# Routing the mixture's rows by a table of tokens, with gathers from GpSimd

## The reference

```python
rn = (xf - mu) * rsqrt(var + EPS) * ln_gamma + ln_beta
probs = softmax(rn @ gate_w.T)
rw, sel = top_k(probs, 2)
comb = sum(one_hot(sel, 8) * rw[..., None], axis=1)
h = gelu(einsum('nc,efc->enf', xf, w1))       # w1: 8 x 1024 x 512
y = einsum('enf,ecf->enc', h, w2)             # w2: 8 x 512 x 1024
x = x + einsum('enc,ne->nc', y, comb)
```

## Time and profile before

| | us |
|---|---|
| median of 3 runs (1031.40 to 1032.46) | 1031.93 |
| profiled execution, device time | 1033.27 |
| its span in the profile | 1031.5 |
| PE busy | 913.2 (89%) |
| DVE busy | 686.1 (67%) |
| ACT busy | 527.9 (51%) |
| POOL busy | 407.2 (39%) |

### The profile page before, as it was taken

The page is one execution under the profiler, slowest core; times in us unless marked ns, Lnnn a source line. Parts: engine busy times, 40 slices in busy tenths (PEclk is TensorE's granted clock), DMA queues, the critical chain, the costliest instruction groups (busy, mean ns, idle before and its releaser), DMA issues. The chain is left out here.

```text
span 1031.5 us, 24517 instructions
## 1 busy us (share of the span) xinstructions
PE 913.2 (89%) x10397; PEld 611.0 (59%) x10397; DVE 686.1 (67%) x1010; ACT 527.9 (51%) x801; POOL 407.2 (39%) x293
## 2 busy tenths in 40 slices
PE   5988999999999999999999999767775495899996
PEld 3464676676676676676676676433443383676663
DVE  7854777646777645777644455775667495799983
ACT  3543445555345545345544345531554562899893
POOL 2020665355665355665345545422230074111112
PEclk9998999999999999999999999669997597999999
DMA  9361122443022332022332022007600355999993
GB/s 340 103 180 42 33 61 60 126 105 89 22 59 63 124 105 54 20 56 63 124 106 53 22 54 62 2 1 263 270 2 1 129 212 171 414 400 398 400 391 45
DMA packets 48455, 134.63 MB, mean 131 GB/s; under 512 B 9870, under 2 KB 11790, under 8 KB 44506
## 3 DMA queue, kind: packets, MB, share of 16 engines
q1 hardware_dynamic: 45356, 126.78, 36.1%
q0 software_dynamic: 2800, 6.04, 2.9%
q10 hardware_dynamic: 192, 0.26, 0.1%
HBM read 94.99 MB, written 11.33 MB: 103 GB/s over the span
## 5 line engine op out<-in xcount | busy, mean ns | idle before, releaser
L419 POOL TENSOR_TENSOR acc_pool<-acc_pool,pT 128x1024 f32<-128x1024 f32 x92 | 216.7, 2355 | 170.2 <-ACT pT L688 168.5
L688 ACT ACTIVATE pT<-ps_s 128x1024 f32<-128x1024 f32 x128 | 130.7, 1021 | 216.7 <-PE ps_s L857 216.4
L526 DVE TENSOR_REDUCE mpart<-ps_b 128x1 f32<-128x512 f32 x256 | 174.4, 686 | 94.7 <-PE ps_b L835 93.6
L819 PE MATMUL ps_a<-wv_hi,cT_hi 128*128 128x128 f16 x1024 | 184.4, 220 | 0.4 <-ACT kbias L608 0.4
L821 PE MATMUL ps_a<-wv_hi,cT_lo 128*128 128x128 f16 x1024 | 183.3, 219 | 0.0
L820 PE MATMUL ps_a<-wv_lo,cT_hi 128*128 128x128 f16 x1024 | 183.2, 219 | 0.0
L521 DVE TENSOR_TENSOR k_lo<-k_f,k_hi 128x512 f16<-128x512 f32 x64 | 72.3, 1129 | 70.2 <-ACT k_hi L664 69.9
L835 PE MATMUL ps_b<-k_stack,q_stack 98*128 98x512 f16 x256 | 98.6, 388 | 11.9 <-DVE mpart L526 7.7
L819 PEld LDWEIGHTS ps_a<-wv_hi,cT_hi 128*128 128x128 f16 x1024 | 99.7, 97 | 12.4 <-issue 11.9
L857 PE MATMUL ps_s<-q_stack,k_stack 98*128 98x128 f16 x1024 | 100.2, 227 | 7.3 <-ACT pT L688 6.2
L820 PEld LDWEIGHTS ps_a<-wv_lo,cT_hi 128*128 128x128 f16 x1024 | 100.2, 98 | 5.0
(11 more groups left out here) (248 smaller groups left out, 1873.9 us busy)
## 6 DMA issues: line engine op xcount, KB each, us to landing
w_raw<-in_w SPq DMA_DIRECT2D x30, 2048.0 KB, 16.8
raw<-in_context SPq DMA_DIRECT2D x16, 1024.0 KB, 5.8
k_stack<-k_hi SPq DMA_DIRECT2D x252, 64.0 KB, 2.0
k_stack<-k_lo SPq DMA_DIRECT2D x128, 64.0 KB, 2.0
slots_in<-a_zeros SPq DMA_DIRECT2D x1, 3855.0 KB, 13.6
rows_in<-slots_in SPq DMA_DIRECT2D x15, 257.0 KB, 16.3
q_stack<-k_stack SPq DMA_DIRECT2D x12, 128.0 KB, 2.4
x_sb<-in_x SPq DMA_DIRECT2D x2, 512.0 KB, 4.1
```

The lines of the kernel that those rows point to most:

```text
L419: nc.gpsimd.tensor_tensor(acc_pool[:, :], pT[:, 0, :] if p == 1 else acc_pool[:, :], pT[:, p % PT, :], ALU.add).then_inc(pool_add, 1)
L526: nc.vector.tensor_reduce(mpart[:, j, kb:kb + 1], bank_b(step)[:, :], AX.X, ALU.max).then_inc(p1_max, 1)
L688: nc.scalar.activation(pT[:, p % PT, :], ps_s[:, :], ACT.Exp, scale=SM_SCALE).then_inc(exp_done, 1)
L819: nc.tensor.matmul(to, cT_hi[:, c, keys], t.wv_hi[:, c, col], start=(c == 0), stop=False)
```

## The change

The features no longer travel with the record. What changes:

- `normed` rows are stored to a new table `rows` in memory, in token order: three blocks during self-attention, the fourth at the start of the mixture, and one block of zeros for the spare token (5 stores of 256 KB).
- The record of a slot is 2 floats, weight and token. The same eight scatters write them into `slots` (1920 x 2 floats), which was filled beforehand from an 8-byte constant per partition.
- POOL waits for the eight, reads `slots` back into one SBUF tile `table` with a plain DMA of its own (128 partitions x 15 tiles x 2 floats), and then gathers each tile's 128 rows out of `rows` by the token column, four tiles ahead.
- SP no longer waits for `sent` and no longer loads rows.
- `y_evict(k - 2)` stands behind `w2_high(k)` in ACT's loop, waits for `table` once, and has three buffers `y`.
- The copy `second` is gone, and so is the load of the spare token's number into the zeros: `misc_in` counts to 5.

```diff
-ROWS_RING = 8
-RECORD = D + 2
+ROWS_RING = 6
+Y_RING = 3
...
# self-attention, SP
-            sp.dma_start(t.normed[:, :, D + 1], io.tokens[:, 0:NB], allow_slow_non_contiguous=True).then_inc(s.tokens_in, 16)
             sp.wait_ge(zeroed, 1)
-            sp.dma_start(io.out[NB * P:NB * P + P, :], zeros[:, 0:D]).then_inc(s.out_sem, 16)
-            sp.dma_start(zeros[:, D + 1:D + 2], io.tokens[:, NB:NB + 1], allow_slow_non_contiguous=True).then_inc(misc_in, 16)
-            sp.wait_ge(misc_in, 16 * 6)
-            sp.dma_start(io.slots_in.rearrange("(n p) d -> p n d", p=P),
-                         zeros[:, :].unsqueeze(1).broadcast_to([P, TILES, RECORD])).then_inc(s.slots_zeroed, 16)
+            sp.dma_start(io.out[NB * P:NB * P + P, :], zeros[:, :]).then_inc(s.out_sem, 16)
+            sp.dma_start(io.rows[NB * P:NB * P + P, :], zeros[:, :]).then_inc(s.rows_stored, 16)
+            sp.dma_start(io.slots.rearrange("(n p) r -> p n r", p=P), io.empty.unsqueeze(1).broadcast_to([P, TILES, 2])
+                         ).then_inc(s.slots_empty, 16)
...
+            for d in range(NB - 1):
+                sp.wait_ge(m_normed, 2 * d + 1)
+                sp.dma_start(io.rows[P * d:P * (d + 1), :], t.normed[:, d, :]).then_inc(s.rows_stored, 16)
...
# self-attention, POOL and DVE
-            v.wait_ge(misc_in, 16 * 6)
+            v.wait_ge(misc_in, 16 * 5)
...
# mixture, SP
+            sp.wait_ge(normed, 2 * NB)
+            sp.dma_start(io.rows[P * EARLIER:P * NB, :], t.normed[:, EARLIER, :]).then_inc(s.rows_stored, 16)
...
             w2_load(2)
-            sp.wait_ge(sent, 16 * 2 * NB)
-            for k in (*range(EARLY, ROWS_AHEAD), *range(EARLY)):
-                rows_load(k)
             experts_of_further_tiles()
-            for k in range(TILES):
-                if k + ROWS_AHEAD < TILES:
-                    rows_load(k + ROWS_AHEAD)
-                if 4 <= k + 3 < TILES:
+            for k in range(1, TILES):
+                if k + 3 < TILES:
                     w1_load(k + 3)
-                if 3 <= k + 2 < TILES:
+                if k + 2 < TILES:
                     w2_load(k + 2)
...
# mixture, POOL
+            def gather(k):
+                if k >= EARLY + ROWS_RING:
+                    pool.wait_ge(x_tr, k - ROWS_RING + 1)
+                nc.gpsimd.indirect_dma_start(
+                    out=rows_in[k % ROWS_RING][:, :], out_offset=None, in_=io.rows, in_offset=token(k),
+                    bounds_check=NB * P + P - 1).then_inc(rows_got[k % ROWS_RING], 16)
...
+            pool.wait_ge(sent, 16 * 2 * NB)
+            pool.dma_start(table[:, :, :], io.slots.rearrange("(n p) r -> p n r", p=P)).then_inc(table_in, 16)
+            pool.wait_ge(s.rows_stored, 16 * (NB + 1))
+            pool.wait_ge(table_in, 16)
+            for k in range(EARLY, ROWS_AHEAD):
+                gather(k)
             pool.wait_ge(s.out_sem, 16 * (NB + 1))
             for k in range(TILES):
+                if k + ROWS_AHEAD < TILES:
+                    gather(k + ROWS_AHEAD)
                 pool.wait_ge(y_out, k + 1)
                 if k:
                     pool.wait_ge(y_added, 16 * k)
...
# mixture, ACT
             def y_evict(k):
                 act.wait_ge(down, k + 1)
-                if k < EARLY:
-                    act.wait_ge(rows_got[k], 16)
-                if k >= 2:
-                    act.wait_ge(y_added, 16 * (k - 1))
+                if k == 0:
+                    act.wait_ge(table_in, 16)
+                if k >= Y_RING:
+                    act.wait_ge(y_added, 16 * (k - Y_RING + 1))
...
             for k in range(TILES):
-                if k >= 2:
-                    y_evict(k - 2)
...
                 if k:
                     w2_high(k)
+                if k >= 2:
+                    y_evict(k - 2)
                 if k + 2 < TILES:
                     w1_high(k + 2)
```

More of the change, by code:

```diff
@@ L946, in self_attention @@
         m_hat, gT = sb("am_hat", [P, D]), sb("am_gT", [P, NC, P])
-        zeros = sb("a_zeros", [P, RECORD])
+        zeros = sb("a_zeros", [P, D])
         ps_p = ctx.enter_context(nc.psum_tensor("a_psp", [P, HEADS, P], F32))
@@ L1367, in mixture @@
                         for half in (t.cT_hi, t.cT_lo)]
-        rows_in = [sb(f"rows_in{u}", [P, RECORD]) for u in range(ROWS_RING)]
+        rows_in = [sb(f"rows_in{u}", [P, D]) for u in range(ROWS_RING)]
         xT_hi, xT_lo = [[sb(f"m_xT_{half}{u}", [P, NC, P], F16) for u in range(2)] for half in ("hi", "lo")]
@@ L1371, in mixture @@
         h_hi, h_lo = [[sb(f"h_{half}{u}", [P, NF, P], F16) for u in range(2)] for half in ("hi", "lo")]
-        y = [sb(f"m_y{u}", [P, D]) for u in range(2)]
-        second = sb("m_second", [P, NB, RECORD])
+        y = [sb(f"m_y{u}", [P, D]) for u in range(Y_RING)]
+        records, table = sb("m_records", [P, 2, NB, 2]), sb("m_table", [P, TILES, 2])
         stats, mv, rstd = sb("m_stats", [P, 6]), sb("m_mv", [P, 2]), sb("m_rstd", [P, 2])
@@ L1485, in _, with token @@
             nc.gpsimd.memset(ones[:, :], 1.0).then_inc(const_in, 1)
-            pool.wait_ge(s.slots_zeroed, 16)
-            pool.wait_ge(rowed, 1)
-            pool.wait_ge(s.tokens_in, 16 * 2)
-            for k, records in enumerate((t.normed, second)):
-                for b in range(NB):
-                    if k:
-                        pool.wait_ge(copied, NB + b + 1)
-                    nc.gpsimd.indirect_dma_start(
-                        out=io.slots_in, out_offset=bass.IndirectOffsetOnAxis(ap=rows[:, k, b:b + 1], axis=0),
-                        in_=records[:, b, :], in_offset=None, bounds_check=TILES * P - 1).then_inc(sent, 16)
+            def token(k):
+                return bass.IndirectOffsetOnAxis(ap=table[:, k, 1:2].bitcast(mybir.dt.uint32), axis=0)
+            def gather(k):
[4 more added lines that the diff above has]
+                    bounds_check=NB * P + P - 1).then_inc(rows_got[k % ROWS_RING], 16)
+            pool.wait_ge(s.slots_empty, 16)
+            pool.wait_ge(rowed, 1)
+            for b in range(NB):
+                for k in range(2):
+                    nc.gpsimd.indirect_dma_start(
+                        out=io.slots, out_offset=bass.IndirectOffsetOnAxis(ap=rows[:, k, b:b + 1], axis=0),
+                        in_=records[:, k, b, :], in_offset=None, bounds_check=TILES * P - 1).then_inc(sent, 16)
+            pool.wait_ge(sent, 16 * 2 * NB)
[4 more added lines that the diff above has]
+                gather(k)
             pool.wait_ge(s.out_sem, 16 * (NB + 1))
             for k in range(TILES):
+                if k + ROWS_AHEAD < TILES:
+                    gather(k + ROWS_AHEAD)
                 pool.wait_ge(y_out, k + 1)
@@ L1502, in _ @@
                     pool.wait_ge(y_added, 16 * k)
-                token = rows_in[k % ROWS_RING][:, D + 1:D + 2].bitcast(mybir.dt.uint32)
                 nc.gpsimd.indirect_dma_start(
-                    out=io.out, out_offset=bass.IndirectOffsetOnAxis(ap=token, axis=0), in_=y[k % 2][:, :],
+                    out=io.out, out_offset=token(k), in_=y[k % Y_RING][:, :],
                     in_offset=None, bounds_check=NB * P + P - 1, compute_op=ALU.add).then_inc(y_added, 16)
@@ L1529, in _ @@
             v.wait_ge(powed, 3 * NB)
-            for k, dst in ((1, hat[:, :]), (0, t.normed[:, last_b, 0:D])):
+            for k, dst in ((1, hat[:, :]), (0, t.normed[:, last_b, :])):
                 nc.vector.tensor_scalar(dst, t.x[:, last_b, :], mv[:, 0:1], rstd[:, k:k + 1],
@@ L1608, in _ @@
             then_wait(nc.vector.tensor_reduce(rows_f[:, :, :], placed[:, :, :, :], AX.X, ALU.add))
-            for k, records in enumerate((t.normed, second)):
-                nc.vector.tensor_scalar(records[:, :, D], weight[:, k, :], UNSCALE, None, ALU.mult)
+            nc.vector.tensor_scalar(records[:, :, :, 0], weight[:, :, :], UNSCALE, None, ALU.mult)
             nc.vector.tensor_copy(rows[:, :, :], rows_f[:, :, :]).then_inc(rowed, 1)
@@ L1702, in _ @@
             w1_high(1)
-            for b in range(1, NB):
-                second_copy(b)
             x_high(0)
             for k in range(TILES):
-                if k >= 2:
-                    y_evict(k - 2)
                 for i in range(2):
@@ L1884 @@
     tiles = np.asarray(inputs["ctx_1024"]).reshape(NB * NKT, P, D)
+    tokens = np.zeros((P, NB + 1, 2), np.uint32)
+    tokens[:, :, 1] = np.arange((NB + 1) * P).reshape(NB + 1, P).T
     arrays = {
@@ L1904 @@
         "before": np.ascontiguousarray(np.stack([np.triu(np.ones((P, P)), 1), np.ones((P, P))], axis=1).astype(np.float16)),
-        "tokens": np.ascontiguousarray(np.arange((NB + 1) * P, dtype=np.uint32).reshape(NB + 1, P).T).view(np.float32),
+        "records": np.ascontiguousarray(np.tile(tokens[:, None, 0:NB, :], (1, 2, 1, 1))).view(np.float32),
+        "empty": np.ascontiguousarray(tokens[:, NB, :]).view(np.float32),
         "counting": np.tile(np.concatenate([np.arange(MORE), P * np.arange(EXPERTS),
```

37 lines of the change are left out of this document (15 added, 22 removed).

## The result

| | before | after |
|---|---|---|
| median of 4 runs, us | 1032.20 (1031.40 to 1033.62) | 1055.55 (1051.17 to 1059.03) |
| profiled execution, us | 1033.27 | 1051.17 |
| its span, us | 1031.5 | 1049.4 |

After takes 1.0223 times as long, 95% interval 1.0181 to 1.0264. Slower was forecast, but by 3 us and within 1047; it is 23 us in the medians and 17.9 us between the two profiled spans. Those 17.9 us can be divided into four stretches of PE's stream. The profiled execution is the fastest of after's four, and that of before lies 1.1 us above its median, so the medians lie further apart than the spans; where the other executions of after lose their 3 to 8 us no trace shows.

What follows compares the result with a forecast made beforehand. The prediction took the DMA engines to bound the middle, PE only 0.4 us a tile behind. Terms -2.4 + 2 + 6.1 - 6.6 + 4.1 = +3.2 us gave a median of about 1035 us; 8 in 10: 1024 to 1047.

Steps and rivals of the forecast that it cites:

- Self-attention, minus 2.4: Self-attention: DVE's first bias addition no longer waits for the spare token's number; the stage moves 2.4 us earlier, bounds 0 and 4.
- The scatters, plus 2: Routing scatters: still eight with POOL's times as before, but the last three land beside weights; 2 us more, bounds 0 and 4.
- Table and gather, plus 6.1: Start of tile 3: two dependent transfers, table load then gather, take 9.1 us against 3.0 for the row load before.
- The table's pieces: Rival, slower: POOL builds the table load's 1920 pieces at scatter pace, 13.5 us more, median about 1049; chance 0.15.
- The stream after it, minus 6.6: Tile 3's transposes to last up product: with a lead in weights PE is the bound, 133.1 us instead of 139.75.
- the third rival: Slower: gathers and results on POOL wait for pauses in DVE's splits, results remain for the end; about 1042, chance 0.12.
- POOL falls behind in the stream: Rival, slower: gathers and results wait for pauses in DVE's splits; end 11 us late instead of 4, about 1042; chance 0.12.
- The results, plus 4.1: End of the kernel: result 12 leaves later behind ACT's last weight split, the last results follow serially in 6.15 us steps.
- The scatters are not held: Rival, faster: fifth and sixth scatters wait for at most one 2.3 us DVE instruction; median about 1023; chance 0.17.

Runs made afterwards that it cites:

- the spare token's experiment: Kernel before, with the load of the spare token's number counted on another semaphore, so VectorE's first bias addition does not wait for it: 0.9986.
- results unchained: Changed kernel, each tile's result written plainly to its own table, without adding or waiting for the landing of the one before: 1.0006, 1031.0 us.
- weights first: Kernel before, with SP issuing w1 of tile 4, w2 of tile 3 and w1 of tile 5 ahead of its wait for the scatters: 1.0036, 1035.46 us.
- pauses: Kernel before, with a one-column VectorE memset behind each weight split of the first tiles: 0.9981, 1027.58 us.
- all three repairs: Changed kernel, gathers seven tiles ahead, `y_evict` ahead of the gelu, VectorE waiting before w2_low(0) until the eight scatters are issued: 0.9972, 1030.73 us.

## Why the prediction was wrong, point by point

*Self-attention, minus 2.4.* The term looks right in the table and was not. The wait went as said, but by the spare token's experiment the gain is given back within self-attention. After's own trace shows the same. DVE starts its first normalisation there at 693.72 instead of 695.92, so 2.2 us early, in code that was not touched. It is 4.4 us early at the first bias addition (701.81), 3.4 at the next (713.87), 3.1 at 729.72, and 2.2 again at 764.39 and at the start of the mixture. So after's 2.2 us stem from before self-attention, and that they nearly equal the forecast is luck; what gave them no run shows. The prediction moved the stage whole ("the stage moves with it"), having read one wait and not the next ones. Its lower bound, 0, is what happened.

*The scatters, plus 2.* Same two holds, of 9.89 and 10.91 us. The 1.2 us more of the sixth and a landing of 6.19 instead of 2.77 us beside the weights make 4.6, over the stated bound of 4. The size was short, the mechanism right (making VectorE wait removes the holds).

*Table and gather, plus 6.1* (its heading says 6.2). From the last landing (865.03) to PE's start it took 8.83 us, 3.0 before: plus 5.8. The table's pieces are no cost: 1.28 us. By the Trainium skill's rule that descriptors are cheap to build ("DMA: Bandwidth & Descriptors", section "Anatomy of one DMA — SWDGE (gpsimd) path"), the sum stayed as it was; the trace agrees for this load.

*The stream after it, minus 6.6.* This is the step that failed, by 11.4 of the 14.7 us between the forecast and the spans. "PE is then the bound" looked only at weights, PE and DVE. It forecast 133.1 us and after took 144.5. Two things were wrong in it, in opposite directions. PE's own step is 10.98 us and not 11.35: seven of after's eleven steps are 10.98 to 11.04, and all eleven with gathers seven ahead. The prediction took 11.35 from PE's busy time and from one step of before, and neither was PE's need. That alone would have made the stream 8.3 + 11 x 10.98 = 129.1 us, and with gathers seven ahead it is 128.6, so the part about the weights' lead held. The other four steps of after hold its four later waits for rows, 11.5 us, and about 4 us more. Of these 3.6 lie behind the two longest waits (steps of 15.68 and 19.18 us around waits of 2.80 and 6.47), where the clock was near half. That 144.5 less 11.5 is again 133.0 is chance: the slow clock and the step that was taken too long happen to be of one size. What was missed is that rows, until then loaded by SP ahead of the weights of the tile before, now sat in POOL's stream behind a wait for a landing. A gather for tile k + 5 is issued when result k has been sent. Result 7 leaves at 975.40, so the gather of tile 12 goes at 977.29, and PE is then at tile 11 (978.24). Results take 11.4 to 14.6 us a step while weights move, and a gather another 9 to 14. Every number for that was in the rows: results landing in 10.9 us, plus 0.8 of POOL, against PE's 11.35. The prediction used them for the third rival and there asked only what stays over for the end. *POOL falls behind in the stream* named the right cause ("a step of results is ... already more than PE's 11.35") and put the price in the wrong place: in the tail, which came out at 4.8 us instead of 11, and not in the rows, and it had 0.12. Where PE no longer waits for rows, with gathers seven ahead, the tail is 10.8 us longer than before (37.0 against 26.2), near the 11 it named. The landing of results also grew, from a median of 10.9 us in before to 10.5 to 13.7 us in after's chain while weights move.

*The results, plus 4.1.* Found 4.8: the last three are back to back, in steps of 7.05 and 5.78 us, where 6.15 each was forecast.

*The scatters are not held.* Not so in after. But the held scatter is not fixed to a place: with results unchained it was the eighth (9.30 us), and in two kernels with the same order on DVE and POOL (weights first, pauses) no scatter after the first took over 2.3 us. By the Trainium skill ("SBUF — State Buffer", section "Who interferes with whom") a hold lasts as long as the running instruction of DVE. Both lengths occur here, 2.3 us, which fits the rule, and 9 to 11 us over four splits in a row, which does not; what decides between them stays open, as no run varied it alone.

What is not settled: of the 23 us in the medians, 17.9 are placed. The rest is mostly that after's other executions are longer than the profiled one.

## What to carry to other kernels

When a transfer is moved to another engine's queue, list what stands ahead of it there and what that waits for, and lay the whole period of that queue (wait, issue, landing) beside the bound's step; a chain of landings that is just slower than the bound costs little until something else queues behind it, a buffer runs out, or it runs on past the bound's end. Take the bound's own step from a stretch in which nothing else is late, not from its busy time. A wait removed is only worth what the next waits leave: read on for two or three of them before moving a stage. And if GpSimd's indirect transfers take long while the DMA engines stand still, look at what VectorE reads, and consider making it wait a few us.

## What the runs showed of the hardware

- An indirect transfer of GpSimd can be held off by several VectorE instructions with two SBUF inputs in a row: scatters of 9.30 to 10.91 us over four weight splits, a gather of 8.02 us over three, where 0.97 to 1.02 us is usual. If those 0.97 to 1.02 us are taken off the end, every such hold ended within 0.15 us of VectorE's next input from PSUM or of its going idle. Having VectorE wait 3.2 us took the long scatters away.
- In after, the landing of a result (128 rows of 2 KB, adding) took 4.3 to 8.6 us when the weights were ending or through and 10.5 to 13.7 us beside them. The median over the fifteen results was 11.2 us there and 10.7 for plain writes with the results unchained. The table of 15 KB landed in 3.8 us in after and, beside weights, in 8.9 with all three repairs.
- After PE had stood 2.80 and 6.47 us in after, its granted clock was 0.53 over the next 1.9 us and 0.50 over the next 1.8. These two steps were together 3.6 us longer than PE's own step and the waits. That step, one tile at a granted clock of 1.00, is 10.98 us.
- A plain load of 1920 pieces of 8 bytes took GpSimd 1.28 us.
